# A fused linear-attention and FP4 feed-forward kernel: output projection spread over attention's later groups, small chains reordered

## The reference

```
q = relu(x @ Wq) * SCALE ; k = relu(x @ Wk) ; v = x @ Wv      # each (b, s, 64 heads, 64)
kv  = einsum('bsid,bsjd->bsdj', k, v)
out = einsum('bsid,bsdj->bsij', q, kv)
q_norm = einsum('bsid,bsd->bsi', q, k.sum(axis=2))
out = (out / (q_norm[..., None] + EPS)).reshape(b, s, 4096) @ Wo + bo
x = layernorm(x + out)
h = silu(fp4(x) @ fp4(w_gate).T) * (fp4(x) @ fp4(w_up).T)
x = layernorm(x + fp4(h) @ fp4(w_down).T)
```

## Time and profile before

| | us |
|---|---|
| median of three runs | 2271.95 |
| the three runs | 2269.57 to 2275.17 |
| the profiled execution, whole | 2271.46 |
| its span, first to last instruction | 2269.7 |
| PE busy | 2050.3 (90%) |
| PE weight loads busy | 1961.0 (86%) |
| DVE busy | 1805.8 (80%) |
| POOL busy | 1690.7 (74%) |
| ACT busy | 1618.7 (71%) |
| mean share of the 16 DMA engines, main queue | 61.9% |

### The profile page before, as it was taken

One profiled execution on the slowest core, in us unless ns is written; L12 is line 12 of the kernel. 1 busy time (PEld: TensorE's weight loads), 2 busy tenths in 40 slices (PEclk: granted clock), 3 DMA queues, 4 the chain that ended last, 5 costly groups with the idle time before them and its releaser, 6 DMA issues.

```text
span 2269.7 us, 88816 instructions
## 1 busy us (share of the span) xinstructions
PE 2050.3 (90%) x37963; PEld 1961.0 (86%) x37963; DVE 1805.8 (80%) x3359; ACT 1618.7 (71%) x3210; POOL 1690.7 (74%) x2192
## 2 busy tenths in 40 slices
PE   4799999999999999999999999999999999999975
PEld 3788998898898898898899899899899889889874
DVE  6778888888888888888888887888888888888873
ACT  4667777777777777777777777777777777777761
POOL 4577787787787787787787778778778778778772
PEclk9999999999999999999999999999999999999996
DMA  6467656666656666756756766765765665665661
GB/s 194 95 133 151 139 127 146 141 130 142 148 125 139 147 132 134 156 126 133 159 124 134 153 132 129 155 133 127 152 137 127 148 141 127 143 146 126 139 130 33
DMA packets 523216, 308.32 MB, mean 136 GB/s; under 512 B 275590, under 2 KB 497734, under 8 KB 522310
## 3 DMA queue, kind: packets, MB, share of 16 engines
q1 hardware_dynamic: 522822, 302.65, 61.9%
HBM read 17.38 MB, written 4.19 MB: 10 GB/s over the span
## 4 chain that ended last, share of the span: by engine, by line
PE 55%; POOL 18%; issue 9%; ACT 9%; DVE 6%; DMA 2%; SPq 0%; DVEq 0%; ACTq 0%; POOLq 0%
PE ps L408 15%; PE ps L361 12%; PE ps L363 12%; PE ps L362 12%; POOL o_st L1078 8%; POOL q_nat L1068 7%; ACT q_bd L564 6%; DVE q L798 3%; PE ps L434 3%; DVE o L816 2%; ACT hqT L571 2%; POOL small L1086 2%; PE ps L445 1%; DMA x_in<-in_L_attn_x 1%; ACT ks L577 1%
## 5 line engine op out<-in xcount | busy, mean ns | idle before, releaser
L1078 POOL TENSOR_TENSOR o_st<-o,o_st 128x256 bf16<-128x256 f32 x1024 | 659.8, 679 | 5.9 <-ACT o_st L639 5.9
L1068 POOL TENSOR_TENSOR q_nat<-q,q_nat 128x512 bf16<-128x512 f32 x512 | 590.3, 1176 | 33.2 <-ACT q_nat L597 32.9
L639 ACT CAST o_st<-o 128x256 bf16<-128x256 f32 x1024 | 358.4, 403 | 214.8 <-DVE o L816 211.0
L361 PE MATMUL ps<-v_st,q_bd 128*128 128x66 bf16 x4096 | 456.3, 198 | 42.9 <-DVE o L816 37.5
L361 PEld LDWEIGHTS ps<-v_st,q_bd 128*128 128x128 bf16 x4096 | 419.7, 114 | 61.9 <-DVE o L816 56.3
L362 PE MATMUL ps<-v_st,q_bd 128*128 128x66 bf16 x4096 | 454.0, 198 | 0.0
L363 PE MATMUL ps<-v_st,q_bd 128*128 128x66 bf16 x4096 | 452.5, 197 | 0.0
L816 DVE TENSOR_TENSOR o<-ps,rec 128x512 f32<-128x512 f32 x512 | 344.5, 683 | 120.7 <-POOL o_st L1078 110.2
L362 PEld LDWEIGHTS ps<-v_st,q_bd 128*128 128x128 bf16 x4096 | 417.5, 116 | 0.2 <-issue 0.2
L363 PEld LDWEIGHTS ps<-v_st,q_bd 128*128 128x128 bf16 x4096 | 416.8, 115 | 0.0
L408 PE MATMUL ps<-w_o,o_st 128*128 128x128 bf16 x6144 | 376.9, 220 | 3.4 <-DMA o_st<-swap 3.4
(11 more groups left out here) (129 smaller groups left out, 5334.4 us busy)
## 6 DMA issues: line engine op xcount, KB each, us to landing
q_bd<-q_nat SPq DMA_DIRECT2D x256, 256.0 KB, 3.9
swap<-v_st SPq DMA_DIRECT2D x64, 576.0 KB, 5.1
v_st<-v_st SPq DMA_DIRECT2D x64, 576.0 KB, 5.6
v_st<-swap SPq DMA_DIRECT2D x64, 576.0 KB, 5.4
swap<-o_st SPq DMA_DIRECT2D x64, 512.0 KB, 4.9
o_st<-o_st SPq DMA_DIRECT2D x64, 512.0 KB, 6.8
o_st<-swap SPq DMA_DIRECT2D x64, 512.0 KB, 5.5
x_in<-in_L_attn_x SPq DMA_DIRECT2D x64, 64.0 KB, 5.3
```

The source lines that it names most:

```text
L361: nc.tensor.matmul(dst, lhs(0), rhs(0), start=True, stop=False)
L639: last = nc.scalar.copy(ost[1 - t.par][:, 0, :, a, g * G:(g + 1) * G, :], src[:, a])
L1068: last = nc.gpsimd.tensor_tensor(qnat[:, 1, a, :, e, :], src[:, a], qnat[:, 0, a, :, e, :], ALU.subtract)
L1078: last = nc.gpsimd.tensor_tensor(lo[:, :, a], src[:, a], hi[:, :, a], ALU.subtract)
```

## The change

- PE: `wo_part` 0 stands right after attention group 2 (ahead of group 3), part 1 after q's chunk 2, part 2 after q's chunk 3, part 3 after group 6, part 4 after group 7. `h_transpose` stands one chunk of k sooner, ahead of chunk 2.
- ACT: one of the three `q_stay` copies (the hi half, l=0, a=1) is taken out of the turn's start. A new function `q_stay_next` makes that copy for the tile in front at the end of the turn before, between `norm_o` 7 and `o_hi` 6. `hq_copy` so follows one copy, not two.
- DVE: the steps from `x_max` to `x_norm` stand one place sooner each, `residual_2` stands after `x_grid`, not ahead of `x_top`; the last two reciprocals are taken one by one, and `scale_o` 7 stands ahead of `h_grid`.
- POOL: `x_bias` stands ahead of `x_back`, not between `o_lo` 3 and `q_lo` 2.
- SP: the load of `x_res` stands ahead of the second o move, not after the load of `x_in`.

```diff
--- before.py
+++ after.py
@@ SP
+                if t.mid:
+                    if t.back:
+                        sp.wait_ge(s_r1, t.b + 1)
+                    sp.dma_start(x_res[:, :], x_t[bass.ts(t.m, T), :]).then_inc(s_xres, 16)
                 if t.mid:
                     move(o4[t.par], osw, s_oswap, om[1], 1)
...
-                if t.mid:
-                    if t.back:
-                        sp.wait_ge(s_r1, t.b + 1)
-                    sp.dma_start(x_res[:, :], x_t[bass.ts(t.m, T), :]).then_inc(s_xres, 16)
@@ PE
+                h_transpose(t)
                 project(t, "k", 2)
-                h_transpose(t)
                 project(t, "k", 3)
...
                 out_group(t, 2)
+                wo_part(t, 0)
                 out_group(t, 3)
                 project(t, "q", 2)
+                wo_part(t, 1)
                 out_group(t, 4)
                 out_group(t, 5)
-                wo_part(t, 0)
-                wo_part(t, 1)
                 project(t, "q", 3)
+                wo_part(t, 2)
                 out_group(t, 6)
-                wo_part(t, 2)
+                wo_part(t, 3)
                 out_group(t, 7)
-                wo_part(t, 3)
                 wo_part(t, 4)
@@ ACT
+            def q_stay_next(t):
+                if not t.front:
+                    return
+                if t.attend:
+                    act.wait_ge(s_done["out"], (t.o + 1) * NG)
+                else:
+                    act.wait_ge(s_clear, 2)
+                act.wait_ge(s_qhi, (t.n + 1) * NC)
+                nc.scalar.copy(qbd[64:128, 0, :, 1, HALF:DH, :].rearrange("p k e s -> p k (e s)"),
+                               qnat[64:128, 0, 1].rearrange("p k e s -> p k (e s)")).then_inc(s_qstay, 1)
...
                 q_stay(t, 1, 0)
-                q_stay(t, 0, 1)
                 hq_copy(t)
...
                 norm_o(t, 7)
+                q_stay_next(t)
                 o_hi(t, 6)
@@ DVE
                 v_lo(t, 3)
+                x_max(t)
                 k_add(t, 1)
-                x_max(t)
+                x_scale(t)
                 k_add(t, 2)
+                x_recip(t)
                 x_lo(t)
-                x_scale(t)
+                x_norm(t)
                 k_add(t, 3)
-                x_recip(t)
-                x_norm(t)
-                residual_2(t)
                 x_top(t)
...
                 x_grid(t)
+                residual_2(t)
...
-                recip(t, 6, 2)
+                recip(t, 6, 1)
                 scale_o(t, 6)
+                recip(t, 7, 1)
+                scale_o(t, 7)
                 h_grid(t)
-                scale_o(t, 7)
@@ POOL
                 q_stay(t)
+                x_bias(t)
                 x_back(t)
...
-                x_bias(t)
                 q_lo(t, 2)
```

## The result

| | median us | of runs | ratio to before | 95% interval |
|---|---|---|---|---|
| before | 2270.95 | 4 | | |
| changed | 2472.33 | 4 | 1.088 | 1.086 to 1.091 |

The change makes the kernel 201 us slower, 8.8%. The forecast was 2420 us, in a range of 2350 to 2500. The profiled execution of the changed kernel has a span of 2468.5 us; PE is busy 85% of it.

The account below looks back on a forecast made before the run. PE nearly alone bounded the turn; the change would close a loop of 4.11 + 14.41 + 17.6 = 36.1 us against 33.72. 62 turns x 2.4 = 149 us on 2271.5 gave 2420 us, range 2350 to 2500.

Parts of the forecast that it names:

- The closed loop: Third o move's landing, part 0, group 3, `norm_o` 3, `q_hi` 1, POOL, next o moves: 36.1 us a turn against 33.72.
- Landing to `q_lo` 1, 4.11: From the third o move's landing through part 0, group 3 and `q_hi` 1 to `q_lo` 1's start: 4.11 us.
- POOL's run, 14.41: POOL from `q_lo` 1 to the next first o move: 14.87 us, less 0.46 for `x_bias`, is 14.41.
- The moves, 17.6: Three chained o moves, first issue to last landing: 17.3 us by medians and issues, plus 0.3 for `x_res`.
- `x_res` among them: 64 KB load ahead of the second o move: taken as +0.3 us, between -0.3 and +2.3 if its issue is slow.
- The turn, +2.4: Each of 62 turns becomes 36.1 us instead of 33.72, 2.4 us longer.
- What `h_transpose` and the chain of x give: PE's 1.1 us wait at `down` goes; `k_sum` is late next, with a wait of 0.3 to 0.7.
- `k_add` 3 ... does not move: On DVE, `k_add` 3 keeps its time, ending at 1055.31 + 1.22; the last fold tied to it ends about 1.05 sooner.
- Alone that is worth at most 1.05 us a turn: The earlier fold and `k_sum` would save PE at most 1.05 us a turn; inside the loop, nothing.
- `q_stay_next` at nothing: The copy between ACT's `norm_o` 7 and `o_hi` 6 costs nothing, being covered by idle time; at most 1.9 us otherwise.
- Rival 1: The o moves land in time, needing 15.2 us; gain 0 to 28 us, 2243 to 2272; chance 0.07.
- The fit weighed in the prediction: 2.0 us plus bytes at 436 GB/s: 3.2 us per 512 KB move, 9.6 for three, no wait at part 0.

Follow-up runs that it names:

- run 2: Kernel before with only the five output projection parts moved to their new places on PE: 2434.32 us, ratio 1.071.
- run 1: Changed kernel with the five output projection parts back at their old places on PE: 2284.06 us, ratio 1.006.
- run 5: Changed kernel with the three o moves issued ahead of the three v moves, `x_res` between the second and third o move: 2283.01 us, ratio 1.005.
- run 7: Changed kernel with the `x_res` load back behind `x_in` and `x_bias` back between `o_lo` 3 and `q_lo` 2: 2444.23 us, ratio 1.075.
- run 8: Changed kernel with the output projection parts at their old places and attention group 1 ahead of `k_sum` on PE: 2263.42 us, ratio 0.996.
- run 4: Changed kernel with 32 extra matmuls on PE between group 2 and part 0: 2474.39 us, ratio 1.090.

## Why the prediction was right, and where it was off

**The closed loop: right, shown.** It was forecast from a slack, 2.2 us between the landing and part 0 in the turn read the earlier trace rows (3.2 on average of 60 turns), and from three orders written in the code. The parts alone cost 163 us (run 2), taking them back gave 188 (run 1), and making the moves land sooner gave 189 with PE's order untouched (run 5).

**Landing to `q_lo` 1, 4.11, and POOL's run, 14.41: right.** 18.52 was forecast, 18.55 measured in turns at full clock (4.06 and 14.49, taken apart), and with `x_bias` left in, 18.97 (run 7) and 18.95 (run 2) against 18.98.

**The moves, 17.6: too small by 0.3.** They took 17.92. The mis-sized part is `x_res` among them, taken at 0.3 from its bytes; run 7 shows 0.8, on moves of 17.14 without it where the sum had 17.3. Bytes were the wrong measure. In the changed kernel issuing the second move takes 1.7 us on average, in run 7 it takes 0.6, so a slow issue, which the bound of 2.3 stood for, seems to be part of the cost; that bound was too high.

**The turn, +2.4: measured +3.1.** Of the missing 0.7 some 0.3 is the moves and 0.4 the clock. The forecast took full clock for granted after reading it in one turn, and did not ask what a 2 to 4 us wait of PE does to it. 22 turns lost 1.2 us each in the loop, some 26 us; the 9 at `k_sum` lost little, as the wait at part 0 absorbed them. With 60 turns: 60 x 3.14 = 189 of the 201 us. In the two profiled executions, 199 us apart, the one turn ahead of the 60 and the two behind them took 13 us more, and what lies before the first o move and after the last took 3 less. The clock was no term of the sum; that 2472 still lies inside the range is owed to the room left there for longer moves, not to a forecast of it.

**What `h_transpose` and the chain of x give: step right, value wrong.** The wait at `down` went and `k_sum` took its place; the forecast said 0.3 to 0.7 there, and it is 1.0. Of its terms, "`k_add` 3 ... does not move" is wrong: with the steps of x ahead of it, DVE starts it 0.55 us behind the last matmul of k's chunk 3, before 0.04 (averages of the middle turns), and the fold follows `k_add` 3 in 1.97 us, not 2.79. So the fold ends only 0.3 sooner, while PE comes 1.1 sooner. "Alone that is worth at most 1.05 us a turn" holds but misleads: alone, with the half clock that the moved wait brings, these edits lose 13 us (run 1). **`q_stay_next` at nothing**: run 1's 33.45 us a turn leaves no room for a large cost of it, but no run took it alone.

**Rival 1** was priced nearly right: with the landing in time, the edits other than the moves' order gave 33.89 a turn (run 5), no gain over 33.77, as "eaten by part 0's own matmuls" said. The 2283 us lie 11 above its range, since `q_lo` 1 starts 19.4 us behind the first o move, before 18.9: the gain ahead of `k_sum` was smaller than part 0's matmuls.

**The fit weighed in the prediction**, which the Trainium skill, "DMA: Bandwidth & Descriptors", section "Anatomy of one DMA — SWDGE (gpsimd) path", states for the other issue path, gives an estimate of 3.2 us for a move and 9.6 for three. It does not carry over to these: even with v's moves behind them the three take 14.6 (run 5). The prediction's reason, v's moves on the same engines, accounts for 17.9 against 14.6 and not for the rest, which stays open.

## What to carry to other kernels

Before an input's user is moved forward, read how long ago the input had landed, not whether the user waits: a slack of some 2 to 3 us that no list of waits shows decided 200 us here. Where a wait is put ahead of work for which engines wait in a ring (here PE, ACT, POOL, DMA and PE again), add up the ring; if it is longer than the bounding engine's own turn, it is the new turn. And a wait on PE can cost more than its length, when it is long or close to another one, since what follows can run at 1.2 GHz.

## What the runs showed of the hardware

TensorE's granted clock fell to 0.50 after PE had been idle for 2.59 us at part 0, and also after waits of 1.21 and 0.52 us with some small f32 matmuls between them. It did not in every turn that had them: in the changed kernel it fell at part 0 in 22 turns with waits of 2.0 to 4.3 us, and not in 29 with waits of 0.6 to 2.9. It fell in none of the 60 turns of the kernel before, whose waits of 1.1 and 0.5 lay some 5 us apart. Such a stretch cost 1.75 us a turn in run 1, and 1.2 us of the loop at part 0 in the changed kernel. Filling PE's wait with useful work (run 8, 19 turns to none) or with matmuls of no use (run 4, 22 turns to one) took it away at that place. In run 4 more turns fell to it at `k_sum`, and why is not known.

The same three moves of 512 KB took 14.6 us with v's moves behind them (v's first runs beside the third, and the 64 KB load of `x_res` stands between the second and the third). They took 17.1 to 17.4 with v's moves between them, and 17.9 to 18.5 with the 64 KB load ahead of the second as well. The DMA engines' share was 0.72 while they ran in a turn of run 5 (953.26 to 967.10), and 0.95 in one of the changed kernel (1034.45 to 1051.49).
